# A graph network of three convolutions: fifteen dense tiles kept instead of fourteen, fewer register loads, narrower packing products

## The reference

```python
h = maximum(layernorm(x), 0)
x = x + gcn(gcn(h, W1, b1), W2, b2)      # two convolutions, linear in h
h = maximum(layernorm(x), 0)
# third convolution, with a filter per edge
C = 0.5 * (cos(edge_weight * pi / 5) + 1) * (edge_weight < 5)
Wf = (silu(edge_attr @ mlp_w1 + mlp_b1) @ mlp_w2 + mlp_b2) * C[:, None]
agg = segment_sum((h @ lin1_w)[src] * Wf, dst) / maximum(count(dst), 1)
x = x + silu(agg @ lin2_w + lin2_b) @ lin_w + lin_b
# gcn(x, W, b): y = x @ W; out[dst] += y[src] * dinv[src] * dinv[dst]; out + b
```

## Time and profile before

| | |
|---|---|
| three runs, median | 1401.13 us (1399.64 to 1403.17) |
| the profiled execution | 1403.79 us, of which its span 1402.0 |
| head, up to the first gather | 65.6 us |
| first pass, first gather to last window | 65.6 to 660 us |
| second pass, first gather to last window | 667 to 1101 us |
| busy: PE, POOL, DVE, ACT | 1238.9, 1034.1, 923.8, 581.0 us |

### The profile page before, as it was taken

One profiled execution on the slowest core, in us unless ns is written; L12 is line 12 of the kernel. 1 busy time (PEld: TensorE's weight loads), 2 busy tenths in 40 slices (PEclk: granted clock), 3 DMA queues, 4 the chain that ended last, 5 costly groups with the idle time before them and its releaser, 6 DMA issues.

```text
span 1402.0 us, 36567 instructions
## 1 busy us (share of the span) xinstructions
PE 1238.9 (88%) x12470; PEld 1082.1 (77%) x12470; DVE 923.8 (66%) x3249; ACT 581.0 (41%) x1289; POOL 1034.1 (74%) x1039
## 2 busy tenths in 40 slices
PE   5357999999999998995699999999996798999996
PEld 2246888988988887894699999999996465676674
DVE  7986777787878885875255566466555454565564
ACT  6657665676665674661133224223210111221221
POOL 9777777777777776775777777777777477777773
PEclk9956999999999999996799999999998698989997
DMA  5346677667777776678778878968867424535532
GB/s 140 96 129 182 187 219 208 207 206 211 207 208 200 213 208 182 201 210 234 211 216 251 245 213 248 262 198 244 260 179 196 112 64 121 120 93 120 121 97 62
DMA packets 260404, 255.29 MB, mean 182 GB/s; under 512 B 136277, under 2 KB 217866, under 8 KB 259319
## 3 DMA queue, kind: packets, MB, share of 16 engines
q1 hardware_dynamic: 217335, 165.00, 40.8%
q0 software_dynamic: 42880, 87.88, 23.5%
HBM read 182.45 MB, written 70.31 MB: 180 GB/s over the span
## 4 chain that ended last, share of the span: by engine, by line
PE 56%; POOL 19%; issue 9%; DVE 6%; ACT 4%; DMA 4%; ACTq 2%; SPq 0%; DVEq 0%; POOLq 0%
PE ps_product L2145 27%; POOL ring_parts L1077 19%; PE ps_pack L2119 8%; PE ps_banks L2101 8%; PE ps_banks L2083 4%; ACT adjacency L1229 3%; ACT packed_T L1278 1%; DMA ring_parts<-node_table,src_idx 1%; PE ps_banks L2189 1%; DMA ring_parts<-node_table,packed_src 1%; PE ps_pack L2127 1%; DMA edge_in<-in_edge_attr_dram 1%; PE ps_banks L2285 1%; DVE z_nodes L1454 1%; PE ps_node L2170 1%
## 5 line engine op out<-in xcount | busy, mean ns | idle before, releaser
L2145 PE MATMUL ps_product<-adjacency,table_parts 128*128 128x232 bf16 x4704 | 551.3, 264 | 0.0
L1077 POOL DMA_INDIRECT ring_parts<-node_table,src_idx x384 | 380.9, 992 | 143.4 <-issue 112.4
L1077 POOL DMA_INDIRECT ring_parts<-node_table_parts,src_idx x384 | 392.7, 1023 | 122.4 <-issue 114.9
L2145 PEld LDWEIGHTS ps_product<-adjacency,table_parts 128*128 128x128 bf16 x4704 | 458.5, 99 | 6.9
L1229 ACT CAST adjacency<-ps_banks 128x550 f32 x504 | 337.4, 669 | 266.7 <-PE ps_banks L2101 212.3
L1077 POOL DMA_INDIRECT ring_parts<-node_table,packed_src x216 | 206.1, 954 | 80.3 <-issue 64.6
L2101 PE MATMUL ps_banks<-code_onehot,lo_onehot 128*128 128x400 bf16 (+2 forms) x1494 | 235.3, 267 | 27.7 <-ACT adjacency L1229 21.5
L1631 DVE TENSOR_SCALAR code_onehot<-code_iota,code_T 128x600 bf16<-128x600 bf16 x504 | 183.1, 386 | 59.5 <-PE ps_banks L2101 57.4
L2101 PEld LDWEIGHTS ps_banks<-code_onehot,lo_onehot 128*128 128x128 bf16 x1494 | 150.7, 116 | 76.7 <-issue 29.0
L1278 ACT COPY packed_T<-ps_pack 67x96 f32 x416 | 98.1, 236 | 220.7 <-PE ps_pack L2119 173.1
L2119 PE MATMUL ps_pack<-pack_onehot,edge_in 128*67 128x96 f32 x1664 | 171.0, 252 | 12.8 <-DMA edge_in<-in_edge_attr_dram 6.5
(11 more groups left out here) (282 smaller groups left out, 1360.9 us busy)
## 6 DMA issues: line engine op xcount, KB each, us to landing
kept_tiles<-adjacency SPq DMA_DIRECT2D x98, 406.0 KB
adjacency<-kept_tiles SPq DMA_DIRECT2D x98, 406.0 KB
edge_in<-in_edge_attr_dram SPq DMA_DIRECT2D x207, 128.0 KB
packed_attr<-packed_T SPq DMA_DIRECT2D x8, 864.0 KB, 8.2
adjacency<-packed_attr SPq DMA_DIRECT2D x6, 1152.0 KB, 9.2
ring_parts<-node_table,src_idx POOLq DMA_INDIRECT x384
ring_parts<-node_table_parts,src_idx POOLq DMA_INDIRECT x384
node_table_parts<-table_parts SPq DMA_DIRECT2D x7, 672.0 KB
```

Source lines behind the costliest of these rows:

```text
L1077: gps.indirect_dma_start(to, None, rows, bass.IndirectOffsetOnAxis(index, 0)).then_inc(gathered[s], 16)
L2145: product = mm(ps_product[:, 0:COLS], table_parts[:, k, part, :], adjacency[:, buffer_of(c, tile), k, :], start=(k == 0 and part == 0), st ...
```

## The change

It does five things. The late tiles are 0, 6 and 12 in place of 0, 5, 10 and 15, so that 15 tiles are kept: the first pass has 103 slots, 16 builds and 15 products, the second 82 slots as before, with two builds in place of three. ACT loads all 28 columns of a tile at its first chunk, and the places of four groups at once, in place of loading them slot by slot. In a pack, the second chunk of a pair comes first with 96 columns, and the first chunk follows with 56; the head tests in addition that no first chunk has over 56 edges. In the head, DVE scales 2 blocks of 7 and ACT 5. The half of the one-hot buffer goes by a count that runs on over both passes, since 103 is odd.

```diff
-LATE_TILES = (0, 5, 10, 15)
+LATE_TILES = (0, 6, 12)
+PACK_FIRST = 56
+COLUMN_LOAD, PLACE_LOAD = 28, 4
-    TABLE_BLOCKS = 3
+    TABLE_BLOCKS = 2
...
             pair_totals = total_row.rearrange("a (c t) -> a c t", t=2)
+            count_over(pair_totals[:, :, 0:1], PACK_FIRST)
...
-            def chunk_columns(chunks):
-                if not chunks:
-                    return []
-                tile, first = chunks[0][1:]
-                at = tile * TILE_CHUNKS + first
-                _, columns = nc.values_load_multi_w_load_instructions(
-                    chunk_at[0:1, at:at + len(chunks)], engines=[ACTIVATION], min_val=0, max_val=COLS - SPAN,
+            def load_columns(chunks):
+
+                for m, tile, q in chunks:
+                    if q % COLUMN_LOAD:
+                        continue
+                    at = tile * TILE_CHUNKS + q
+                    _, loaded = nc.values_load_multi_w_load_instructions(
+                        chunk_at[0:1, at:at + COLUMN_LOAD], engines=[ACTIVATION], min_val=0, max_val=COLS - SPAN,
...
+            def load_places(batch):
+
+                for q in batch:
+                    if q % PLACE_LOAD:
+                        continue
+                    _, loaded = nc.values_load_multi_w_load_instructions(
+                        pack_at[0:1, q * CHUNKS:(q + PLACE_LOAD) * CHUNKS], engines=[ACTIVATION],
...
-                for k in range(CHUNKS):
-                    pair = k // PACK_PAIRS
-                    last = mm(packed_columns(batch.index(q), pair), edge_in[:, s, k, :],
-                              pack_onehot[:, q % 2, k, :], start=(k % 2 == 0), stop=(k % 2 == 1))
+                for pair in range(PACK_PAIRS):
+                    to, k = packed_columns(batch.index(q), pair), 2 * pair
+                    mm(to, edge_in[:, s, k + 1, :], pack_onehot[:, q % 2, k + 1, :], start=True, stop=False)
+                    last = mm(to[:, 0:PACK_FIRST], edge_in[:, s, k, :], pack_onehot[:, q % 2, k, 0:PACK_FIRST],
+                              start=False, stop=True)
```

More of the change, by code:

```diff
@@ L1208, in _, with copy_chunk @@
             nc.scalar.copy(inv_out, ps_pack[0:NB, 0:P]).then_inc(W12_ready, 1)
-            def chunk_columns(chunks):
-                if not chunks:
-                    return []
-                tile, first = chunks[0][1:]
-                at = tile * TILE_CHUNKS + first
-                _, columns = nc.values_load_multi_w_load_instructions(
-                    chunk_at[0:1, at:at + len(chunks)], engines=[ACTIVATION], min_val=0, max_val=COLS - SPAN,
-                    skip_runtime_bounds_check_because="the fast path has been tested for it")
-                return columns
-            def copy_chunk(b, m, tile, q, at):
+            columns, places = {}, {}
+            def load_columns(chunks):
[5 more added lines that the diff above has]
+                        chunk_at[0:1, at:at + COLUMN_LOAD], engines=[ACTIVATION], min_val=0, max_val=COLS - SPAN,
+                        skip_runtime_bounds_check_because="the fast path has been tested for it")
+                    columns.clear()
+                    columns.update({m + i: column for i, column in enumerate(loaded)})
+            def copy_chunk(b, m, tile, q):
                 n = SPAN if q == TILE_CHUNKS - 1 else SPAN - 1
@@ L1313, in fast_path @@
                             split_high(2 * n + 1)
-                        for chunk, column in counted[0:1]:
-                            copy_chunk(b, *chunk, column)
+                        for chunk in counted[0:1]:
+                            copy_chunk(b, *chunk)
                         for q in packs:
-                            pack_out(q, packs, places[q])
-                        for chunk, column in counted[1:]:
-                            copy_chunk(b, *chunk, column)
+                            pack_out(q, packs)
+                        for chunk in counted[1:]:
+                            copy_chunk(b, *chunk)
                         if c == 2 and update_at(plan, n - 1) is not None:
```

30 lines of the change are left out of this document (14 added, 16 removed).

## The result

The change is slower. Three runs took 1422.72 to 1432.06 us with a median of 1426.2, against 1401.13 before; the ratio is 1.0176 (95% interval 1.0147 to 1.0204), far outside the 0.3% that can be told from no change. The blind forecast was 1383.

A forecast was written before the change was run, and what follows sets the result against it. PE was taken to bound both passes, in the first nearly tied with POOL. First pass -7.8 and second -10 made -17.8 us: 1403.8 to 1386.0, less 2.7 for the median, 1383; 8 in 10 for 1360 to 1406.

The forecast's parts named there:

- Head: Start of the kernel: first gather at about 64 instead of 65.6 us, taken as -1.5 us (0 to -2).
- Products and builds: First pass, product stretch: PE gains 147 matmuls and 28 chunks and loses seven windows, +20.2 us.
- PE's units: Costs on PE: 99 ns a product matmul, 0.29 us a chunk, 0.35 a window, 0.69 a group's pack.
- Packs: Product stretch: narrow matmuls take 60 ns, saving 92 ns in each of 128 packs, -11.8 us (0 to -17.9).
- Register loads: ACT in the product stretch: loads take 59 us for 98, of which PE gets back -6 us.
- PE may run two chunks ahead, which hides most of that: Product stretch: PE's lead hides most of the delay from long column loads, so -6 us was taken.
- +17: Product stretch: cost if a 1.7 us load ahead of a tile's first copy held PE each time, 15 x (1.7 - 0.55).
- the clock gives the change nothing to win: Both passes: PE's granted clock is already 0.99 and 1.00 of 2.4 GHz, so no gain from it.
- Tail: First pass behind the products: last window at 651.5 against 659.3 us, -7.8 with the head's part in it.
- Second pass: PE loses 14.4 us of chunks and packs, POOL stands next at 11.5; taken as -10 us (0 to -11.5).
- ACT paces the builds: Rival, first pass: 28 more copies cost ACT 20.9 us instead of PE's 8.1, total 1414 us; chance 0.12.

The follow-up runs named there:

- before_tiles: The kernel before with only the tiles of the change, fifteen kept, and loads, packs and head as before: 1424.48 us, ratio 1.0162.
- changed_wide: The change with all four matmuls of a pack 96 columns wide, in the old order: 1437.33 us, ratio 1.0258 to the kernel before.
- changed_places1: The change with places loaded one group at a time, still 28 columns in one load: 1415.37 us, ratio 1.0101 to the kernel before.
- changed_columns_once: The change with the first tile's columns loaded once and used for all tiles, places one group at a time: 1391.48 us, 0.9928 of the kernel before.

## Why the prediction was wrong, step by step

Taken in a row, the product stretch goes from 492.5 us by the tiles to 525.5 (`before_tiles`), by the new loads to 539.5 (`changed_wide`, which has the new head as well) and by the narrow packs to 525.1: +33.0, +14.0 and -14.4, where the forecast had +20.2, -6 and -11.8.

- **Head** (-1.5): the first gather came at 64.2, as worked out; by slot 12 the 1.4 us were gone again (140.4 for 139.3).
- **Products and builds** (+20.2): right as PE's units, wrong as the stretch. With fixed columns PE is busy 477.4 us for 467.9 before, +9.5 where 20.2 - 11.8 = 8.4 was forecast for tiles and packs; but with loaded columns the tiles alone made the stretch 33.0 us longer. A build was counted as PE's 8.1 us; that 28 more copies need their columns loaded, in six fewer slots, was left to a rival.
- **Packs** (-11.8): near for PE, whose busy time fell by 8.4 to 14.2 us. In the changed kernel they give 539.5 - 525.1 = 14.4 us of stretch; in the kernel before only 4, since POOL stands next, and with the new tiles and the loads of before 4.6, since PE then waits for ACT.
- **Register loads** (-6): the step that failed, with the wrong sign. The durations away from stores were right, 1.73 us and 1.0. Their effect was not: "PE may run two chunks ahead, which hides most of that" fails where two loads stand one behind the other and the second falls into the store of the finished tile: 1.7 + 2.2 to 2.8 us, a stall of 3 us, and a lower clock behind it. By themselves the loads cost 14 us in the kernel before and 12 in the change. Much of it is the clock: with the pair parted (`changed_places1`) PE idles as long, but is busy 7 us less. That "the clock gives the change nothing to win" was right, but what a wait can lose by it was left out. +17 had been the upper bound; the value was taken from the other end because of 7 us of loads on the chain. The row that should have warned was there: column loads of 0.55 us in the median reached 5.37, and nothing was asked about what ran beside them.
- **Tail** (18.8 us long): 21.6. **Second pass** (-10): -8.4, and POOL's waits fell to 2.1 us as said. The extra kept tile took the DMA share to 0.84 (forecast 0.83), and a gather in the first pass no longer.
- **The rival "ACT paces the builds"** (1414, chance 0.12) named the right engine and place. Its means, ACT's busy time, is not borne out: 34 us more of it cost 4.6 us of stretch, 12 us less gave nothing. What the runs tie the loss to is ACT's register loads, and a part of it to how long they last beside the stores.

The cause, as far as runs show it: the tile that saves seven gathers puts 28 more copies to loaded columns on ACT, in slots that PE's own work fills, and one more tile to store. Long loads in a lump cost 1.3% of the time (1.0176 to 1.0050). Of the rest, the stores' effect on the loads holds 1.1% at most (1.0050 to 0.9940, where the second pass has lighter transfers too; 11.4 us are in the first pass). Without column loads the same tiles take 0.9911, 1388 us beside a forecast of 1383: the sum of PE's units stood, the feeding of PE did not. Four things stay open: how the rest, from 0.9940 to 0.9911, divides between short loads, register arithmetic and ACT's time as such; why less zeroing on ACT gave nothing; whether small stores would also take the stalls out of the change itself, with its long loads, which wasn't run; and whether stores issued at other times would give the 1.1% back, which wasn't tried.

## What to carry to other kernels

Before giving more work to the bound engine in exchange for less on the second, sum the third that feeds it, slot by slot, with its register loads and not its busy time alone: ACT showed 318 busy us of 493 and yet held PE. For an operation whose longest duration is ten times its median, find out what runs beside the long ones before pricing it by the median, here a store to memory. A saving on one engine pays only up to whatever stands next: the narrow packs gave 4 us of the stretch alone, where POOL stood next, 4.6 with the new tiles, where PE went on to wait for ACT, and 14 with the new loads. And price a wait of the matmul engine with what its clock does behind it: with the new loads alone PE idled 5 us longer, and took 9 us longer for the same matmuls.

## What had not been expected of the hardware

- Loads of contiguous registers in whole fours take 0.31 us for four and 1.73 for 28, 62 to 77 ns each; four with a stride take 0.89, 224 ns each, and five contiguous ones took 1.15. The Trainium skill ("Runtime: NRT & Kernel Launch", section "Instruction fetch mechanics") has about 200 ns a register for bulk loads as well, on a page that means loads from the chip's main memory, HBM; the loads here read on-chip memory, and come near it only with a stride or not in whole fours.
- Register loads from on-chip memory get longer behind the issue of a tile's store: four registers 0.31 us and up to 1.5, sixteen 1.0 and up to 2.8; with the stores at a seventh of their size, the place loads of four never took over 0.37 at a slot's head, or 0.64 behind copies.
- A copy to a fixed place takes 635 ns, to a column in a register 668, and a register operation of 46 ns stands ahead of the latter. Where that operation fell away, as the columns stayed the same (`changed_columns_once`), a copy took 638.
